# A four-layer kernel on one core: the first layer's tile steps, group ends and tail rearranged, and its decay rows fetched in more transfers

## The reference, cut to what matters

```python
# layer 0, first branch: a state space model, 64 heads of 8, chunks of 128 tokens
zxbcdt = x @ W_in.T                       # z | xBC | dt
xBC = silu(causal_conv(xBC, conv_w))      # 4 taps
dt = softplus(dt_raw + dt_bias);  a = dt * -exp(A_log);  cum = cumsum(a)   # in a chunk
Lmat = exp(where(tril, cum_i - cum_j, -inf))          # per head
Yd = einsum(C.B * Lmat * dt, xs)                      # inside a chunk
Yoff = exp(cum) * C . S_prev;   S = S * exp(cum_end) + states   # over the chunks
y = (Yd + Yoff + D * xs) * silu(z);  out = rmsnorm(y) * norm_w @ W_out.T
# layer 0, second branch: 8 experts of 128 units, the best 2 of each token, and a shared one of 512
x = x + first(xn) + routed(xn) + shared(xn)
# layer 1: attention, and a feed-forward whose weights are ternary:
scale = mean(abs(w));  w_ternary = clip(round(w / scale), -1, 1)
```

## Time and profile before

| | |
|---|---|
| median of 3 runs | 1669.21 us |
| the profiled execution | 1666.6 us |
| its span | 1664.9 us |
| mean granted clock of PE | 0.895 |
| busy: PE, DVE, ACT, POOL | 80%, 55%, 32%, 25% |
| layer 0 (its last instruction ends) | 672.2 us |
| layer 1's block starts | 675.0 us |

### The profile page before, as it was taken

How to read it: one execution, slowest core, us unless ns; L and a number is a source line. 1 busy time by engine, 2 the same in 40 slices (tenths; PEclk the granted TensorE clock), 3 DMA queues, 4 the chain that set the end, 5 groups by cost and what they waited for, 6 DMA issues and landing times. The chain is left out here.

```text
span 1664.9 us, 21457 instructions
## 1 busy us (share of the span) xinstructions
PE 1332.4 (80%) x7251; PEld 823.5 (49%) x7251; DVE 914.0 (55%) x1888; ACT 535.9 (32%) x885; POOL 409.2 (25%) x380
## 2 busy tenths in 40 slices
PE   5556787779777675799999987998655599988987
PEld 3334544554455344457766744544343264644564
DVE  4755455536553766512211378988867435557434
ACT  1444336623752362221212222332302122233321
POOL 3267214512443365200040011000013500000035
PEclk9776999999999877899999988999855698999999
DMA  9122112210222122300000060000001200111113
GB/s 356 51 85 92 36 29 74 80 28 27 94 63 60 37 98 72 113 0 1 0 0 0 0 228 0 0 1 0 1 3 38 83 19 20 32 39 57 55 48 114
DMA packets 68240, 88.83 MB, mean 53 GB/s; under 512 B 15334, under 2 KB 51494, under 8 KB 67497
## 3 DMA queue, kind: packets, MB, share of 16 engines
q1 hardware_dynamic: 61996, 70.76, 12.9%
q0 software_dynamic: 6144, 16.79, 3.3%
HBM read 61.14 MB, written 26.38 MB: 53 GB/s over the span
## 5 line engine op out<-in xcount | busy, mean ns | idle before, releaser
L387 PE MATMUL l_banks<-l_xnT,all_region_a 128*128 128x512 f32 x288 | 131.5, 612 | 0.0
L1819 PE MATMUL l_banks<-l_xnT,mid_region_c 128*128 128x512 f32 (+1 forms) x192 | 96.2, 654 | 17.5 <-DVE l_xnT L2002 17.5
L853 POOL TENSOR_TENSOR all_region_b<-all_region_b,l_lc 128x512 f32<-128x512 f32 x64 | 84.8, 1344 | 83.2 <-DMA all_region_b<-l_lc_rows 83.1
L2662 POOL TENSOR_TENSOR l_rstd<-l_moments,all_neg_half 128x4 f32<-128x4 f32 x20 | 20.6, 1030 | 337.5 <-DVE l_moments L2702 337.5
L867 POOL TENSOR_TENSOR l_rw<-l_xdt,l_decay 128x512 f32<-128x512 f32 x64 | 69.9, 1120 | 76.0 <-DVE l_xdt L1104 76.0
L387 PEld LDWEIGHTS l_banks<-l_xnT,all_region_a 128*128 128x128 f32 x288 | 56.0, 197 | 65.2 <-issue 63.7
L387 PE MATMUL l_banks<-all_region_a,l_xa 128*128 x234 | 68.8, 414 | 20.6 <-issue 14.1
L1124 DVE TENSOR_TENSOR all_region_b<-all_region_b,l_cbd 128x512 f32<-128x512 f32 x64 | 65.7, 1028 | 19.4 <-ACT all_region_b L696 15.4
L1819 PEld LDWEIGHTS l_banks<-l_xnT,mid_region_c 128*128 128x128 f32 (+1 forms) x192 | 37.7, 202 | 68.3 <-issue 49.5
L696 ACT ACTIVATE all_region_b<-all_region_b 128x512 f32<-128x512 f32 x64 | 69.2, 1081 | 4.3
L1077 DVE SCALAR_TENSOR_TENSOR l_xbc<-l_pre,all_cols,l_xbc 128x512 f32<-128x512 f32 x72 | 61.6, 856 | 5.8 <-issue 0.4
(11 more groups left out here) (442 smaller groups left out, 2860.9 us busy)
## 6 DMA issues: line engine op xcount, KB each, us to landing
all_region_b<-l_lc_rows SPq DMA_DIRECT2D x64, 256.0 KB
l_xa<-slots_in SPq DMA_DIRECT2D x39, 128.0 KB, 3.2
slots_out<-l_xa SPq DMA_DIRECT2D x39, 128.0 KB, 3.3
mid_vector_rows<-slots_in SPq DMA_DIRECT2D x39, 128.0 KB, 2.1
slots_out<-all_region_a SPq DMA_DIRECT2D x39, 128.0 KB, 1.7
slots_in<-l_xp SPq DMA_DIRECT2D x4, 1024.0 KB, 12.7
all_region_a<-l_gate_up SPq DMA_DIRECT2D x1, 4096.0 KB, 14.4
all_x<-x SPq DMA_DIRECT2D x4, 512.0 KB, 6.0
```

Of the source, the lines that this page charges most:

```text
L387: return nc.tensor.matmul(out, lhsT, rhs, start=start, stop=stop, **kw)
L853: nc.gpsimd.tensor_tensor(bc[:, k, :, :], bc[:, k, :, :], spread(lc[:, c, heads], 1, BLK), ALU.subtract).then_inc(dd_ready.sem, 1)
L1819: return nc.tensor.matmul(out, lhsT, rhs, start=start, stop=stop)
L2662: nc.gpsimd.tensor_tensor(rstd[:, :], moments[:, :, 1], mem.neg_half[:, 0:GT], ALU.pow).then_inc(rstd_ready.sem, 1)
```

## The change: what it does

- Each piece of decay rows comes by four transfers of 32 partitions instead of one of 128.
- Five of group 0's six convolutions go ahead of routing, between the early transposes.
- In group g > 0 the first projection is ahead of the sums, and the last projection out of group g-1 is behind the sums and ahead of the other nine. DVE's part of it is behind convolutions 0 and 1. The sums take a bank in turn.
- A chunk 0 takes the state's part ahead of its first strip product; the next state is a function of its own.
- A tile step's order is: turn rows of f, gate and up of f-1, down of f-3, turn h of f-2 (banks in that order); ACT takes the turned rows first; the owner of the next tile is loaded behind the gate product. The steps begin at chunk 3 of group 0, and six places have two.
- Scatters 8 to 15 are put by two tiles among POOL's work of chunks 0 and 1; fetches have a buffer for each row, so none waits for an add. All adds are behind the pieces of group 3's chunks.
- The folds, the sums of |w|, ternary weights, and the first group's normalisation for layer 1 are made in layer 0: the first three from chunk 1 of group 3 on, the folds behind the last assemble. Layer 1 starts with PE's transposes. Some of layers 1 to 3's tiles lie in the first layer's buffer `xa`.

```diff
         def decay_rows(g, c, k):
-            rows = spread(lc_d[g, k, c].rearrange("(q n) -> q n", q=NB), 1, BLK)
-            sp.dma_start(bc[:, k, :, :].rearrange("p i h -> p (i h)"), rows).then_inc(bc_landed[k], 16)
+            for q in range(NB):
+                rows = lc_d[g, k, c].rearrange("(q n) -> q n", q=NB)[q:q + 1, :].broadcast_to([BLK, BLK * PH])
+                sp.dma_start(bc[q * BLK:(q + 1) * BLK, k, :, :].rearrange("p i h -> p (i h)"), rows).then_inc(
+                    bc_landed[k], 16)
...
-    places = [(g, c, k) for g in range(GROUPS - 1) for c in range(NCH) for k in range(PIECES) if (g, c) >= (0, 2)]
-    places = sorted(places + [places[-1], places[-3]])
+    places = [(g, c, k) for g in range(GROUPS - 1) for c in range(NCH) for k in range(PIECES) if (g, c) >= (0, 3)]
+    places = sorted(places + [places[4 * i + 6] for i in range(STEPS - len(places))])
...
-        back = (("gu", f - 1), ("th", f - 2), ("dn", f - 3), ("tx", f))
+        back = (("tx", f), ("gu", f - 1), ("dn", f - 3), ("th", f - 2))
... # tensor
         for g in range(GROUPS):
-            sums(g)
             if g > 0:
                 pe.wait_ge(xnT_dve.sem, xnT_dve.done(0, GROUPS - 1 + g))
                 pe.wait_ge(xnT_act.sem, xnT_act.done(0, GROUPS - 1 + g))
-                for j in range(CONV_BLK + Z_BLK):
+                in_proj(g, 0)
+            sums(g)
+            if g > 0:
+                out_proj(g - 1, NCH - 1)
+                for j in range(1, CONV_BLK + Z_BLK):
                     in_proj(g, j)
...
+                if (g, c) == (GROUPS - 1, 2):
+                    pe.wait_ge(weight_sum, 1)
+                    jobs.wait_room(pe, 0, "weight_mean")
+                    jobs.fill(mm(jobs.bank("weight_mean")[:, 0:2], ones[:, :], wabs[:, :]), "weight_mean")
                 assemble(g, c)
-            out_proj(g, NCH - 1)
+        pe.wait_ge(l1.fold_sem, 16 * 2)
+        fold("w_qk", 0, l1.qkv[:, DK:2 * DK, :])
+        fold("w_vo", 2 * DK, l1.out)
+        out_proj(GROUPS - 1, NCH - 1)
+        fold_biases()
... # scalar, at the end of a chunk
+                if (g, c) == (GROUPS - 1, 1):
+                    act.wait_ge(l1.sem, 16 * 2)
+                    for i, part in enumerate((l1.w1, l1.w2)):
+                        last = nc.scalar.activation(below, part.rearrange("p a n -> p (a n)"), ACT.Abs,
+                                                    accum_out=wabs[:, i:i + 1])
+                        act.drain()
+                    act.drain().then_inc(weight_sum, 1)
... # gpsimd
+        late = {0: ((8, 9), (10, 11)), 1: ((12, 13), (14, 15))}
         for g in range(GROUPS):
+            if g == 0:
+                for t in range(2 * GT):
+                    scatter(t)
             if g == GROUPS - 1:
                 for t in range(2 * GT):
                     fetch(t)
             differences(g, 0)
+            if g == GROUPS - 1:
+                for t in range(2 * GT, 3 * GT):
+                    fetch(t)
             weigh(g, 0)
...
                 if c + 1 < NCH:
                     differences(g, c + 1)
+                    for t in ahead:
+                        scatter(t)
                     weigh(g, c + 1)
                 if c > 0:
                     out_scale(g, c - 1)
                 gate(g, c)
+                for t in behind:
+                    scatter(t)
                 if g == GROUPS - 1:
-                    for t in range(2 * GT + 2 * c, 2 * GT + 2 * c + 2):
+                    for t in ((12, 13), (14,), (15,), ())[c]:
                         fetch(t)
... # vector
+            for j in range(2 * n - 2, min(2 * n, EARLY_CONVS)):
+                conv(0, j)
...
         for g in range(GROUPS):
-            for j in range(CONV_BLK):
+            for j in range(EARLY_CONVS if g == 0 else 0, CONV_BLK):
                 conv(g, j)
-                if g == GROUPS - 1:
-                    add(j)
+                if g > 0 and j == 0:
+                    out_stats(g - 1, NCH - 1)
+                if g > 0 and j == 1:
+                    out_add(g - 1, NCH - 1)
...
             take_y(g, NCH - 1)
             out_add(g, NCH - 2)
-            out_stats(g, NCH - 1)
-            out_add(g, NCH - 1)
-        add(TILES - 2)
-        add(TILES - 1)
+        normalise(0, xn, 1)
+        take_folds()
+        quantise(1)
+        out_stats(GROUPS - 1, NCH - 1)
+        out_add(GROUPS - 1, NCH - 1)
+        take_biases()
```

More of the change, by code:

```diff
@@ L229, in layer0 @@
         names += [("in", g, j) for j in range(CONV_BLK + Z_BLK)]
+        names.insert(len(names) - (CONV_BLK + Z_BLK - 1 if g > 0 else 0), ("sums", g))
         for u in range(SHARED):
@@ L245, in layer0 @@
     for g in range(GROUPS):
-        order += [(("sums", g), 7), (("since", g), 3), (("until", g), 2), (("all", g), 1)]
+        order += [(("since", g), 3), (("until", g), 2), (("all", g), 1)]
         order += [(("bc", g, 0), 7), (("bc", g, 1), 7), (("bc", g, 2), 7), (("out", g, 0), 7), (("bc", g, 3), 7)]
@@ L483, in tile_step @@
                 jobs.fill(last, ("tx", f))
+                if f == 0:
+                    owner_of(0)
+            if 0 <= f - 1 < MOE_TILES:
+                i = f - 1
+                if i == 0:
+                    pe.wait_ge(w.moe_sem, 32)
+                jobs.wait_room(pe, 0, ("gu", i))
+                pe.wait_ge(xgT_ready.sem, xgT_ready.done(0, i))
+                for k in range(DK):
+                    part = w.gate_up[:, bass.ds(expert[i] * DK + k, 1), :]
+                    last = mm(jobs.bank(("gu", i))[:, 0:2 * P], xgT[i % 2][:, k, :], part.rearrange("p a n -> p (a n)"),
+                              k == 0, k == DK - 1)
+                jobs.fill(last, ("gu", i))
+                owner_of(i + 1)
+            if 0 <= f - 3 < MOE_TILES:
+                i = f - 3
+                jobs.wait_room(pe, 0, ("dn", i))
+                pe.wait_ge(hT_ready.sem, hT_ready.done(0, i))
+                part = w.down[:, bass.ds(expert[i] + SHARED, 1), :]
+                jobs.fill(mm(jobs.bank(("dn", i))[:, 0:DIM], hmT[i % 2], part.rearrange("p a n -> p (a n)")), ("dn", i))
+            if 0 <= f - 2 < MOE_TILES:
+                i = f - 2
+                pe.wait_ge(h_ready.sem, h_ready.done(0, i))
+                jobs.wait_room(pe, 0, ("th", i))
+                jobs.fill(nc.tensor.transpose(jobs.bank(("th", i))[:, 0:P], hm[i % 2], ident[:, :]), ("th", i))
         def by_tokens(g, c):
@@ L904, in _ @@
                     fetch(t)
-            if g == 0:
-                for t in range(2 * GT):
-                    scatter(t)
             differences(g, 0)
+            if g == GROUPS - 1:
+                for t in range(2 * GT, 3 * GT):
+                    fetch(t)
             weigh(g, 0)
-            if g == 0:
-                for t in range(2 * GT, 3 * GT):
-                    scatter(t)
             for c in range(NCH):
+                ahead, behind = late.get(c, ((), ())) if g == 0 else ((), ())
                 if c + 1 < NCH:
                     differences(g, c + 1)
+                    for t in ahead:
+                        scatter(t)
                     weigh(g, c + 1)
@@ L1535, in _ @@
     def _(act):
-        act.wait_ge(w.sem, 16 * 4)
-        for i, part in enumerate((w.w1, w.w2)):
-            last = nc.scalar.activation(below[:, :], part.rearrange("p a n -> p (a n)"), ACT.Abs,
-                                        accum_out=wabs[:, i:i + 1])
-            act.drain()
-        act.drain().then_inc(weight_sum, 1)
         with act.Fori(0, BATCH) as b:
@@ L3112, in start_up @@
     w.out = take(Z_BLK, DIM)
+    mem.v_bias, mem.q_bias = w.out[:, 0, :], take(1, DK)[:, 0, :]
     take = Taker(mem.region_b)
```

249 lines of the change are left out of this document (120 added, 129 removed).

## The result

The changed kernel takes 1613.2 us (median of four runs, 1611.3 to 1622.4), the kernel before 1669.3 in the same set (four runs, 1664.4 to 1669.6): ratio 0.968, 95% interval 0.9646 to 0.9715. It is faster, as forecast, and inside the range (1560 to 1632), but 24 us behind the 1589 of the sum, and outside the 1572 to 1608 that the forecast gave the likeliest case alone. The profiled execution is the slowest of the four, 1622.4 us, 9 above the median. The 44.2 us divide as follows. T is the end of a group's last assemble, "down" PE's first down product of a group.

The account below looks back on a forecast made before the run. No engine is full; time lies where PE, busy 80%, waits: convolutions, group ends, tile-step stalls, layer 1's preparation. Terms 20 + 36.5 + 4 + 12.5 + 0.5 - 1 + 8 = 80.5 us off 1669.2 gave 1588.7; range 1560 to 1632.

Parts of the forecast that it names:

- the likeliest case: Whole kernel: the summed terms hold, about 1589 us, own range 1572 to 1608; chance 0.66 together with D.
- Group 0: Group 0: first down product about 13 us earlier, then GpSimd's queue paces the chunks; gain 20 us, bounds 10 and 25.
- Ends of groups: Group boundaries: first projection right at T; 10.5 us twice, 17 cut to 15.5 ahead of group 3; 36.5 us, bounds 20 and 42.
- First chunk of a group, transfers in four: Chunk 0: no wait for VectorE's bank, 2 us per group; decay pieces landing 2.0 us apart, not 2.6: 2 us in group 3.
- Tile steps: Expert-tile steps: new order saves 0.65 us each, 2.5 + 10 + 10; doubled steps cost 10 back; net 12.5, bounds 0 and 30.
- Group 3's chunks: Group 3: moved adds under half on the path, ScalarE's w1 wait replaces a VectorE stall; -0.5 us, bounds -9 and +12.
- ScalarE's 11 us for w1: Group 3: ScalarE asks for w1 at about 623, gets it at 634; assemble(3,2)'s copy comes at 643.9 instead of 638.3.
- Tail and layer 1: End of layer 0: folds and last work cost 1 us; layer 1's first projection comes 8 us earlier.
- C: Rival, slower: GpSimd's blocks of eight operations hold VectorE 9.0 us in each of twelve chunks, 108 us, 1697; chance 0.03.
- D: Rival: the four transfers per piece are issue-bound, even late; 4 to 8 us lost, about 1595; 0.66 shared with the forecast.
- B: Rival, more comes: closed holes keep PE's clock up and hide the owner's load, another 10 + 8 + 10 us, 1560; chance 0.11.
- A: Rival: ScalarE bounds the steps, group 0 gives only 12, ends 28, group 3's chunks lose 2; 1625 us; chance 0.20.

Follow-up runs that it names:

- only_ends: Kernel before with only the ends of groups rearranged (first projection ahead of the sums, last projection out behind), adds left between group 3's convolutions: 1640.6 us, ratio 0.985.
- late_gaps: Changed kernel with each group 3 chunk's adds behind its last strip product and a drain behind each GpSimd difference and weigh operation: 1594.9 us, ratio 0.958.

## Why the prediction was right, and where it was not

- *Group 0.* The opening came as worked out (down at 75.3, forecast near 77; 15.3 us), but PE's chunks didn't follow. POOL was on time: its last weighing was due at 155.8 and ended at 159.0. The state product of chunk 3 was due at 156.5 and came at 168.3, behind the product held until 159.6. With pauses in POOL's blocks T is at 178.8, 180.9, 183.4 and 183.7 us in four kernels, without them at 186.2 to 186.9 in four; the forecast was 179.3. So the queue was added up rightly, and the step that failed is that VectorE passes freely beside it: pauses give back 2.5 to 8 us.
- *Ends of groups.* 36.8 us for 36.5. The chain, VectorE's place in it and the 17 - 1.5 ahead of group 3 were right. only_ends adds that the last term hangs on the adds' move.
- *First chunk of a group, transfers in four.* Chunk 0 of group 3 wasn't 2 us shorter but 2.3 longer: PE waited 5.9 us for the weighing, not the 1.5 that the prediction had. Without the four transfers 4 to 5 us are lost, but none of them in group 3, where the 2 us were put.
- *Tile steps.* The gross term was right in its total (26 by the working, 26.7 measured alone), with luck in how the stretches add up. Doubled steps were priced at 2.5 us and cost 3.8; in group 1 gain and price cancel, as forecast, each of them being half as large again. Group 2 gave 3.8 us for 12, where the order alone gave 8.0. In the changed kernel more waits for the transposes remain (10.1 us over all steps, 3.9 with the order alone, 26.6 before); that this is the rest isn't shown, and group 2 varies by 6 us with the same code.
- *Group 3's chunks* is the step that failed, -0.5 against +19.7. "Fewer than half on the path" took the adds as 10 us of work. In the kernel before, the adds of eight tiles (not ten, as the description says) stood ahead of the chunks, those of six behind the last strip of chunks 1 to 3, and two at the end. Between the strips nearly all are on the path, 15.2 us, and there they meet POOL's differences; behind the last strip, where VectorE waits for the projection out, all sixteen cost some 4. The prediction quoted the rule of the port pair for this very pair and named it as speaking against the change, but gave it no price in the sum (whose terms here, 2 + 1 + 1 less 2 + 2, make 0 and not the -0.5 that it uses). The other half of that item, ScalarE's 11 us for w1, is 1.02 us in the changed kernel, but 9.30 in late_gaps, where PE waits 5.06 us behind it (5.6 forecast). So it was seen rightly, and stayed hidden as long as the chunk before was slow.
- *Tail and layer 1.* 5.4 for 7. The folds fill PE's wait as forecast, layer 1's transposes start 0.05 us after its first operation. But VectorE's last operation of layer 0 ends at 633.67 and layer 1's first starts at 639.20, 5.5 us of nothing, where 3.6 lay between the same two before (672.2 to 675.7).
- *The rivals.* C, the slower one, was priced rightly (9.0 us; 9.03 for the 9.72 us product) and came in part: six operations last 33 us beyond their medians, in four chunks, and removing them and the adds' place gives 24.2 us in one set. Its chance of 0.03 was for twelve; that it would come by half belonged into the likeliest case. D fell, B wasn't seen. A's mechanism fell (the order of the steps alone gives 22 us, the ends 36.8), but its time, 1625, lies nearer to the 1613 measured than 1589 does. That the result is inside the range is owed to the room that the range left for A, which stood for other reasons than the ones that came.

The Trainium skill, "SBUF — State Buffer", section "SBUF: two separate sides", says who starts first holds the port pair for its whole instruction. The runs agree that one waits for the other, and add what it means in a row of instructions: with back-to-back operations on POOL the holder doesn't let go (9.72 us for eight), with a drain between them VectorE is let in. Who starts first they don't settle: the held operations at 149.87 and 552.60, and the one of the earlier trace rows, are recorded 0.09 to 0.13 us ahead of POOL's first, those at 545.76 and 605.02 1.4 behind it. So the stall of the earlier trace rows fits the page less closely than the prediction says.

## What to carry to other kernels

Before work is moved on an in-order engine, look at what the engine was doing in the old place and in the new one: sixteen adds cost 4 us in a wait and 15 between products that another engine waits for. If two engines share a port, price the collision for every operation that comes to lie beside the other's longest uninterrupted run, and break that run up. A pause made of a drain cost more where an indirect transfer stood just ahead, so look at what is in flight there. And a queue that is full moves its delay with it: taking 9.8 us from one chunk gave 9.5 to the next. Last, measure how much the same code varies between two profiles before a stretch is read as a gain.

## What the hardware showed

- A drain behind each GpSimd operation costs 0.16 us and turns holds of 8 to 10 us into ones of 2 at most for a strip product. With an indirect transfer just ahead it costs 0.5 to 4.5 us: in group 3 GpSimd goes on 0.2 to 1.0 us after the rows have landed.
- Holding depends on 1 or 2 us of timing, so one kernel can have it or not: chunk 1 of group 3 took 18.2 us or 26.6 with the same code.
- Four transfers of 64 KB for one of 256 KB raise the DMA share from 0.26 to 0.50 to 0.59, and SyncE issues one each 0.47 us.
- The hole between the two layers' blocks was 5.5 us without the drains and 1.3 with them (late_gaps: VectorE from 610.91 to 612.21). Seven drains in GpSimd's list made this difference of 4.2 us in the same way in each of the four kernels that had them; why, stays open.

```profile
612.21 1.41 DVE L1704 BATCH_NORM_STATS2 l_stats<-all_x 128x6 f32<-128x256 f32 x4 [1.29 <-PEq L3199]
```
